# Weights times gathered adapter factors: factors stationary, weights streamed by 512 columns, sums turned by TensorE; last block row by row

## What is computed

```python
def _L0_cond_ref(x, adapter_mapping, W, b, lora_As, lora_Bs):
    base_out = jnp.einsum('bti,oi->bto', x, W) + b
    A = lora_As[adapter_mapping]
    Bm = lora_Bs[adapter_mapping]
    lora_h = jnp.einsum('bti,bir->btr', x, A)
    lora_out = jnp.einsum('btr,bro->bto', lora_h, Bm)
    return base_out + lora_out * SCALING        # SCALING = 2
def _L1_cond_ref(x, adapter_ids, base_weight, base_bias, lora_A_w, lora_B_w):
    ...                                         # the same with its own weights, no scaling
x = x + _L0_cond_ref(x, itok_B_0_23, ...)
x = x + _L1_cond_ref(x, itok_B_6_15, ...)
```

## Time and profile before

| | us |
|---|---|
| median of 3 runs | 307.51 (307.34 to 307.9) |
| the profiled execution | 307.65 |
| its span | 306.1 |
| PE busy in the span | 300.6 (98%) |
| PE weight loads busy | 250.5 (82%) |
| DVE busy | 194.5 (64%) |
| ACT busy | 89.4 (29%) |

### The profile page before, as it was taken

How to read it: one execution, slowest core, us unless ns; L and a number is a source line. 1 busy time by engine, 2 the same in 40 slices (tenths; PEclk the granted TensorE clock), 3 DMA queues, 4 the chain that set the end, 5 groups by cost and what they waited for, 6 DMA issues and landing times.

```text
span 306.1 us, 4010 instructions
## 1 busy us (share of the span) xinstructions
PE 300.6 (98%) x1429; PEld 250.5 (82%) x1429; DVE 194.5 (64%) x327; ACT 89.4 (29%) x143; POOL 18.5 (6%) x43
## 2 busy tenths in 40 slices
PE   7999999999999999999999999999999999999995
PEld 6888898888887688888888888888888888888884
DVE  5777624894749450499998487486485585585312
ACT  4555534012023302392234232231321222231000
POOL 2433130000000010000000000000000000000000
PEclk9999999999999999999999999999999999999999
DMA  7996160000000055504161540641721611702002
GB/s 274 376 350 237 40 167 20 0 0 2 0 0 3 16 177 208 173 5 137 55 229 55 164 140 34 200 137 40 209 86 71 217 42 71 224 34 103 2 34 103
DMA packets 14745, 33.94 MB, mean 111 GB/s; under 512 B 2406, under 2 KB 2406, under 8 KB 14727
## 3 DMA queue, kind: packets, MB, share of 16 engines
q1 hardware_dynamic: 13702, 31.60, 30.2%
q0 software_dynamic: 1024, 2.10, 2.3%
HBM read 22.09 MB, written 11.60 MB: 110 GB/s over the span
## 4 chain that ended last, share of the span: by engine, by line
PE 97%; DVE 1%; ACT 1%; issue 0%
PE bank L800 29%; PE bank L912 17%; PE bank L911 17%; PE bank L913 17%; PE bank L931 5%; PE bank L812 3%; PE bank L918 2%; PE bank L828 2%; PE bank L889 1%; PE bank L887 1%; PE bank L888 1%; PE bank L814 1%; PE bank L860 1%; PE bank L898 1%; PE bank L884 1%; DVE stage L670 0%
## 5 line engine op out<-in xcount | busy, mean ns | idle before, releaser
L800 PE MATMUL bank<-w,w_hi 128*128 128x512 f32 x256 | 78.2, 390 | 0.0
L800 PEld LDWEIGHTS bank<-w,w_hi 128*128 128x128 f32 x256 | 47.9, 188 | 10.7 <-issue 0.9
L800 PE MATMUL bank<-w,w_lo 128*128 128x512 f32 x128 | 49.0, 389 | 0.0
L401 ACT CAST xa<-xr 128x512 fp32r<-128x512 f32 x32 | 19.6, 621 | 34.2 <-PE bank L918 15.7
L800 PEld LDWEIGHTS bank<-w,w_lo 128*128 128x128 f32 x128 | 24.0, 188 | 5.0
L912 PE MATMUL bank<-w_lo,w 128*128 128x512 f32 x64 | 25.1, 392 | 0.0
L913 PE MATMUL bank<-w_hi,w 128*128 128x512 f32 x64 | 25.1, 392 | 0.0
L911 PE MATMUL bank<-w_hi,w 128*128 128x512 f32 x64 | 25.0, 391 | 0.0
L912 PE MATMUL bank<-w 128*128 128x512 f32 x64 | 25.0, 391 | 0.0
L911 PE MATMUL bank<-w 128*128 128x512 f32 x64 | 25.0, 391 | 0.0
L911 PE MATMUL bank<-w_hi,xa 128*128 128x512 f32 x64 | 25.0, 390 | 0.0
(11 more groups left out here) (123 smaller groups left out, 502.7 us busy)
## 6 DMA issues: line engine op xcount, KB each, us to landing
xr<-xT SPq DMA_DIRECT2D x32, 256.0 KB, 4.3
out<-stage SPq DMA_DIRECT2D x28, 256.0 KB, 2.0
stage<-W SPq DMA_DIRECT2D x8, 512.0 KB, 5.1
stage<-W1T SPq DMA_DIRECT2D x8, 512.0 KB, 6.2
a<-rb_rows SPq DMA_DIRECT2D x8, 392.0 KB
rb_rows<-a SPq DMA_DIRECT2D x3, 512.0 KB
rb_rows<-b0w SPq DMA_DIRECT2D x3, 512.0 KB
out<-rows SPq DMA_DIRECT2D x4, 256.0 KB, 2.8
```

The costliest lines, as they stand in the source:

```text
L401: nc.scalar.copy(x_op(j, 0), raw(j)).then_inc(op_hi[j], 1)
L800: return mm(d_bank(m, h)[:, :], left[:, m, k * P:(k + 1) * P], right[:, k, h * HALF:(h + 1) * HALF], start=start, stop=stop)
```

## The change

G is no longer made tile by tile. Its transpose is summed in banks 6 and 7: the gathered factors are stationary and the weights stream by 512 columns (`gt_pass`), 48 products in all. ACT copies the two banks to SBUF (into `c_rows`, made taller, seen as `gt_raw`), PE turns them in eight transposes of 128 x 128 against the identity, and DVE copies the result to `g_all` (`g_copy`). The 128 products of `aux`, its copies and its additions go.

The order changes too. PE does D's tiles 0, 4 and 1 up to block 6, then the 48 products, then block 7 of the three tiles, one tile after the other, so that tile 0 is ready before tile 1. The transposes follow, then S and T, then D tiles 5, 2 and 6 with nothing between them. A1's split moves ahead of block 6's on ACT and DVE, with a semaphore of its own; POOL's loop becomes two, all of A1 first, then all of B0.

```diff
-        c_rows = sb("c_rows", [32 + B, D], F32R)
+        c_rows = sb("c_rows", [P, D], F32R)
...
+        gt_raw = c_rows[:, :].bitcast(F32)
...
-            sp.wait_ge(aux_done, AUX_ST + 1)
+            sp.wait_ge(t_summed, 1)
...
@@ -310,11 +316,13 @@
 
             pool.wait_ge(idx_landed, 2 * DMA)
             with pool.Fori(0, B) as b:
-                i0, i1 = adapter(b), adapter(b + B)
+                i1 = adapter(b + B)
                 pool.dma_start(a1_raw[:, bass.ds(b * BR, BR)],
                                A1T[bass.ds(i1, 1), :, :, :].rearrange("s p k r -> p (s k r)")).then_inc(lora_landed, DMA)
+            with pool.Fori(0, B) as b:
+                i0 = adapter(b)
                 pool.dma_start(b0t_raw[:, bass.ds(b * BR, BR)],
-                               B0T[bass.ds(i0, 1), :, :, :].rearrange("s p k r -> p (s k r)")).then_inc(lora_landed, DMA)
+                               B0T[bass.ds(i0, 1), :, :, :].rearrange("s p k r -> p (s k r)")).then_inc(b0t_landed, DMA)
...
-            def high_lora():
-                act.wait_ge(lora_landed, 2 * B * DMA)
-                for src, to in ((a1_raw, a1), (b0t_raw, b0w)):
-                    nc.scalar.copy(to[:, :, 0:BR].rearrange("p k (b r) -> p b k r", b=B),
-                                   src.rearrange("p (b k r) -> p b k r", b=B, k=KT)).then_inc(lora_hi, 1)
-                act.wait_ge(b0_landed, DMA)
-                nc.scalar.copy(b0w[:, :, 2 * BR], b0_raw[:, :]).then_inc(lora_hi, 1)
-
-            def aux_copy(j):
-                act.wait_ge(aux_summed, j + 1)
-                if j >= 1:
-                    act.wait_ge(aux_done, j)
-                n = 2 * BR + 2 if j == AUX_ST else BR
-                nc.scalar.copy(scratch[:, 0:n], banks[6 + j % 2][:, 0:n]).then_inc(aux_copied, 1)
+            def high_factors(n):
+                src, to, landed = ((a1_raw, a1, lora_landed), (b0t_raw, b0w, b0t_landed))[n]
+                act.wait_ge(landed, B * DMA)
+                nc.scalar.copy(to[:, :, 0:BR].rearrange("p k (b r) -> p b k r", b=B),
+                               src.rearrange("p (b k r) -> p b k r", b=B, k=KT)).then_inc(lora_hi, 1)
+                if n == 1:
+                    act.wait_ge(b0_landed, DMA)
+                    nc.scalar.copy(b0w[:, :, 2 * BR], b0_raw[:, :]).then_inc(lora_hi, 1)
+
+            def gt_copy(h):
+                act.wait_ge(gt_summed, h + 1)
+                nc.scalar.copy(gt_raw[:, h * HALF:(h + 1) * HALF], banks[6 + h][:, :]).then_inc(gt_copied, 1)
+
+            def st_copy():
+                act.wait_ge(st_summed, 1)
+                nc.scalar.copy(scratch[:, 0:2 * BR + 2], banks[6][:, 0:2 * BR + 2]).then_inc(st_copied, 1)
 
...
@@ -419,23 +428,19 @@
                 nc.scalar.copy(c11[b % 2], X[:, :]).then_inc(made["c11"], 1)
 
             for k in range(KT):
+                if k == KT - 2:
+                    high_factors(0)
                 high_w(k)
-            high_lora()
-            aux_copy(0)
+            high_factors(1)
+            for h in range(NH):
+                gt_copy(h)
             high_top(0)
-            aux_copy(1)
-            aux_copy(2)
-            aux_copy(AUX_ST)
-            aux_copy(4)
             high_bottom(4)
             high_top(1)
+            st_copy()
             high_bottom(5)
-            aux_copy(5)
             high_top(2)
-            aux_copy(6)
             high_bottom(6)
-            aux_copy(7)
-            aux_copy(8)
             for j in (A11, A21, A12, A22):
                 high_x(j, 0)
 
...
-            def low_lora():
-                for n, (src, to) in enumerate(((a1_raw, a1), (b0t_raw, b0w))):
-                    dve.wait_ge(lora_hi, n + 1)
-                    nc.vector.tensor_tensor(to[:, :, BR:2 * BR].rearrange("p k (b r) -> p b k r", b=B),
-                                            src.rearrange("p (b k r) -> p b k r", b=B, k=KT),
-                                            to[:, :, 0:BR].rearrange("p k (b r) -> p b k r", b=B),
+            def low_factors(n):
+                src, to = ((a1_raw, a1), (b0t_raw, b0w))[n]
+                dve.wait_ge(lora_hi, n + 1)
+                nc.vector.tensor_tensor(to[:, :, BR:2 * BR].rearrange("p k (b r) -> p b k r", b=B),
+                                        src.rearrange("p (b k r) -> p b k r", b=B, k=KT),
+                                        to[:, :, 0:BR].rearrange("p k (b r) -> p b k r", b=B),
+                                        ALU.subtract).then_inc(lora_lo, 1)
+                if n == 1:
+                    dve.wait_ge(lora_hi, 3)
+                    nc.vector.tensor_tensor(b0w[:, :, 2 * BR + 1], b0_raw[:, :], b0w[:, :, 2 * BR],
                                             ALU.subtract).then_inc(lora_lo, 1)
-                dve.wait_ge(lora_hi, 3)
-                nc.vector.tensor_tensor(b0w[:, :, 2 * BR + 1], b0_raw[:, :], b0w[:, :, 2 * BR],
-                                        ALU.subtract).then_inc(lora_lo, 1)
-
-            def g_add(j):
-                dve.wait_ge(aux_copied, j + 1)
-                nc.vector.tensor_tensor(g_all[:, AUX[j], :], banks[6 + j % 2][:, BR:2 * BR], scratch[:, 0:BR],
-                                        ALU.add).then_inc(aux_done, 1)
+
+            def g_copy(h):
+                dve.wait_ge(g_turned, h + 1)
+                nc.vector.tensor_copy(g_all[:, h * KH:(h + 1) * KH, :].rearrange("p k n -> p (k n)"), banks[6 + h][:, :]
+                                      ).then_inc(g_made, 1)
 
...
                 if b >= 2:
...
                 low_w(k)
-            low_lora()
-            g_add(0)
+            low_factors(1)
             low_top(0)
-            g_add(1)
-            g_add(2)
-
-            dve.wait_ge(aux_copied, AUX_ST + 1)
+            for h in range(NH):
+                g_copy(h)
+            low_bottom(4)
+            low_top(1)
+
+            dve.wait_ge(st_copied, 1)
             dve.wait_ge(masks_made, 3)
             nc.vector.tensor_tensor(s_t[:, :], scratch[:, 0:BR], scratch[:, BR:2 * BR], ALU.add).then_inc(st_step, 1)
             nc.vector.tensor_tensor(t_sum[:, :], scratch[:, 2 * BR:2 * BR + 1], scratch[:, 2 * BR + 1:2 * BR + 2],
-                                    ALU.add).then_inc(aux_done, 1)
+                                    ALU.add).then_inc(t_summed, 1)
             dve.wait_ge(st_step, 1)
             nc.vector.tensor_tensor(s_t[:, :], s_t[:, :], same_batch[:, :, :].rearrange("p b r -> p (b r)"),
                                     ALU.mult).then_inc(st_step, 1)
-            g_add(4)
-            low_bottom(4)
-            low_top(1)
             bias_add(0)
             bias_add(1)
             low_bottom(5)
-            g_add(5)
             bias_add(2)
             bias_add(3)
             low_top(2)
-            g_add(6)
...
             bias_add(4)
             bias_add(5)
             low_bottom(6)
-            g_add(7)
-            g_add(8)
             bias_add(6)
             bias_add(7)
             for j in (A11, A21, A12, A22):
...
-            def aux(j):
-                m = AUX[j]
-                if j >= 2:
-                    pe.wait_ge(aux_done, j - 1)
-                bank = banks[6 + j % 2]
-                for k in range(KT):
-                    cols = slice(k * P, (k + 1) * P)
-                    if k == KT - 1:
-                        mm(bank[:, 0:BR], w0_lo[:, m, cols], a1[:, k, 0:BR], start=False, stop=False)
-                    last = mm(bank[:, 0:2 * BR], w0_hi[:, m, cols], a1[:, k, :], start=(k == 0), stop=(k == KT - 1))
-                    if k < KT - 1:
-                        mm(bank[:, 0:BR], w0_lo[:, m, cols], a1[:, k, 0:BR], start=False, stop=False)
-                last.then_inc(aux_summed, 1)
+            def gt_pass(h, k):
+                cols = slice(h * KH, (h + 1) * KH)
+                bank, at = banks[6 + h], slice(k * P, (k + 1) * P)
+                mm(bank[:, :], a1[:, k, 0:BR], w0_hi[:, cols, at], start=(k == 0), stop=False)
+                mm(bank[:, :], a1[:, k, 0:BR], w0_lo[:, cols, at], start=False, stop=False)
+                return mm(bank[:, :], a1[:, k, BR:2 * BR], w0_hi[:, cols, at], start=False, stop=(k == KT - 1))
 
...
 
-            for k in range(1, KT):
...
@@ -849,31 +845,44 @@
                 for m in TILES[:FIRST_M]:
                     for h in range(NH):
                         d_pass(m, h, k, w0_hi, w1_lo, False, False)
-                        d_pass(m, h, k, w0_lo, w1_hi, False, k == KT - 1)
+                        d_pass(m, h, k, w0_lo, w1_hi, False, False)
+            pe.wait_ge(lora_lo, 1)
+            for h in range(NH):
+                for k in range(KT - 1):
+                    gt_pass(h, k)
+            pe.wait_ge(lo_made, splits(KT - 1))
+            for h in range(NH):
+                gt_pass(h, KT - 1).then_inc(gt_summed, 1)
+            for m in TILES[:FIRST_M]:
+                for h in range(NH):
+                    d_pass(m, h, KT - 1, w0_hi, w1_hi, False, False)
```

(73 more changed lines are left out.)

## The result

| | before | changed |
|---|---|---|
| median of 4 runs, us | 307.58 (307.34 to 307.9) | 304.60 (304.17 to 304.98) |
| ratio | | 0.9909 (95%: 0.9894 to 0.9924) |
| profiled execution | 307.65 | 304.42 |
| its span | 306.1 | 302.8 |

A forecast was written before the change was run, and what follows sets the result against it. PE bounds the kernel: 15.31 us go, 10.89 of factor products and 1.84 of transposes come, so R starts 2.58 earlier. The profiled 307.65 becomes 305.07, the median 305.0 us (range 304.4 to 306.6).

The forecast's parts named there:

- What goes: PE's 128 small G products, 14.77 us at 0.115 each, plus the 0.54 wait before S and T: 15.31 us saved.
- The 48 long products: New factor products of 512 columns on PE, at D's rate of 0.227 us each: 10.89 us added.
- rival 5: Columns alone set a product's cost, so the added products could be cheaper by 0.5: 304.5 us; chance 0.03.
- S and T at 6.66 us later, R 9.24 us nearer to them: S and T start at 52.96 instead of 46.30; behind them 9.24 us of G tiles are gone before R.
- The sum: S and T's delay set against the G tiles gone behind them: R starts at 87.82 instead of 90.40, 2.58 us earlier.
- The transposes: Eight full float32 transposes on PE before S and T, 0.23 us each, 1.84 us in all.
- the floor: ACT and DVE must empty tile 0, then DVE copies G, so S and T cannot start before 52.8 us.
- rival 1: Dearer transposes (0.43 each, 306.5 us) or slower factor products (0.236 each, 305.4 us); chance 0.12 beyond the forecast's small shifts.
- rival 4: Each transpose before S and T costs a whole product of R's kind, 0.86 us: 310.0 us; chance 0.02.
- The covers: Slack claimed to hide A1's earlier split, the gathers, ACT's copies and DVE's work for R; for example 0.25 us before R.
- Rival 3: POOL's turn stays 2.79 us, so B0's gathers come late and S and T start 8.2 later: 313.2 us; chance 0.05.
- Rival 2: PE's clock falls at the transposes, losing 2.92 us as in warm-up: 307.85 us, no change seen; chance 0.03.

The follow-up runs named there:

- the halved columns: Kernel before the change, with 56 of 64 high products of G streaming 128 columns instead of 256: 306.82 us against 307.13 (ratio 0.9995).
- the second profile: The changed kernel run again unchanged, its second profile: 80.20 us from D's first product to R; median of that set 304.88 us (ratio 0.9921).

## Why the prediction was right

- **What goes**, 15.31 us: held. That columns had nearly no part in it is shown by the halved columns; that it was the weight loads is the likely reading, not shown. The Trainium skill (TensorE: Matmul & The Clock Gate, Back-to-back issue gap) gives the formula that the prediction sets against the trace for an isolated gap, and says itself that it leaves out the load; the load's 107 ns stands in the page's next section, LDWEIGHTS.
- **The 48 long products**, 10.89: held (35.53 to 46.41 in the chain, 10.88). Four pieces of 128 columns stream as fast as one of 512, and no faster, so that rival 5 did not come about.
- **S and T at 6.66 us later, R 9.24 us nearer to them**: 6.62 and 9.26, counted from D's first product in the second profile (S and T at 52.66 - 7.30 = 45.36 instead of 38.74; R 34.84 behind them instead of 44.10). The sum, 2.58, came out as 2.64.
- **The transposes were mis-sized**: 0.23 each was said, 0.11 measured (0.87 us for eight in a row). It cost nothing because of the floor that the text named, DVE's path over tile 0: the time between block 7 and S and T is 1.84 us as said, but of 0.87 of turning and 0.97 of waiting. The wait of PE for `g_copy`, said to be at most 0.3, was 0.96. The upper ends of rival 1 and rival 4 thus had no ground. The sum took 52.96 for S and T from PE's own path, and it was DVE's, said to be 52.8, that came out at 52.92 on the same count (7.56 + 45.36); the emptying took the 3.69 us as said (47.81 to 51.50), copy and semaphore 0.83 instead of 0.71. PE's own path would have been ready at 51.12 + 0.87 = 51.99. That a wrong term and the right floor lay within 0.2 us of each other is coincidence, though the text said that they did: by the transposes alone the gain would have come out 0.9 us larger.
- **The covers** held. A turn of POOL's loop takes 1.53 (said 1.52). The last point at which ACT can get A1 was said to be 27.2; with one loop, ACT's start at 30.21 put PE at 34.79, 4.58 later, so that the point is 32.05 - 4.58 = 27.5 (32.05 is when PE needs block 6 if D starts at 7.56). DVE's cover before R's second low part was 1.11 us (said: over 0.25). The transfers of R to D tile 3: DVE is done at 123.29, PE comes at 123.79.
- **Rival 3** did not come about, since a turn got shorter as reckoned. A late gather does cost that kind of price, but by another way than the rival has it. It priced B0, behind block 7; by its own turn of 2.79 us the last A1 would land at 7.99 + 7 x 2.79 + 3.4 = 30.9, after the 27.2, and PE would have waited for block 6 as well. With one loop A1 alone is late enough (30.21) to make the kernel 1.6% slower than before.
- **Rival 2** did not come about: in 14 executions of the changed kernel no mean clock is under 0.998. But it was underrated. The clock falls in the neighbours of this kernel (wait of 1.87 us: 8 of 12 executions; with one loop, where the profile has a wait of 3.41: all four), at 1.53 and 1.9 us in the two traced, where the rival said 2.92. My argument from the wait of 0.54 us did not reach to a wait twice as long behind a stretch of transposes.
- The median lies 0.4 us below the forecast. In the profiled execution 0.6 of the 3.23 us are the early start. Whether the start explains the medians too isn't shown; they differ by 2.5 to 3.0 us from set to set.

## What to carry to other kernels

Where the chain is all PE, count products and not columns: a product that streams 128 or 256 columns against its own 128 x 128 weights cost 0.112 to 0.118 us here, one of 512 columns 0.227. So turning the product round to stream 512, and transposing the sums afterwards, paid even with the transposes. Then look at what follows the transposes: work that doesn't need their result belongs between them and the engine that copies it, and here it saved 1.2 us, nearly half of what the change itself did. And price a wait of PE of some two microseconds at more than its length: 1.87 us let the clock fall in most executions, 0.96 in none of 14; between them nothing was measured.

## What the runs showed of the hardware

- A product of a 128 x 128 stationary operand in `float32r` starts every 0.227 us with 512 columns, every 0.115 with 256 and 128 in turn, and every 0.112 with 128 alone. 128 x 128 float32 transposes in a row take 0.11 each.
- PE's clock fell to the lower level after a wait of 1.87 us behind 1.03 us of transposes in 8 executions of 12, which cost 1.5 us in the one traced; it did not in the six, on another chip, where transposes filled the wait. In both traced falls (waits of 1.87 and 3.41 us) it was still full during the wait and came down when PE was at work again.
- The records give the full granted clock for the first 7 us, although the 13 first products take 0.37 to 0.45 us each on the average of a profile (4.75 to 5.87 us together), up to twice 0.227. The zeros before the change have a median length of 0.628 us, as has a product where the granted clock was 0.50 (0.63, with one loop, 36 to 38 us), while at full clock it has 0.39. So the clock recorded at the start is not a sign of how fast PE runs there; that it is in truth the lower level is likely, not shown.
